# Expert 0's one-hot rows built from 16-bit slot numbers with the channel outermost, and three re-ordered places in the scan stage

## The reference, cut to what matters

```python
# x, ctx: (8, 256, 512); E = 4 experts, H = 2048, capacity 512, TOPK = 2
k, v = layernorm(x), ctx
for t in range(256):                       # one recurrence per sample and channel
    q = max(pp, u + k_t); y_t = (exp(pp-q)*aa + exp(u+k_t-q)*v_t) / (exp(pp-q)*bb + exp(u+k_t-q))
    q2 = max(pp + w, k_t); aa, bb, pp = exp(pp+w-q2)*aa + exp(k_t-q2)*v_t, exp(pp+w-q2)*bb + exp(k_t-q2), q2
x = x + tanh(g_xattn) * y
n = layernorm(x).reshape(2048, 512)
probs = softmax over the top 2 of (n @ Wg + bg)
for i in range(4):                         # the 512 tokens of highest probability for this expert
    sel_p, sel = top_k(where(assigned, probs[:, i], -inf), 512)
    out[sel] += gelu(n[sel] @ W1[i]) @ W2[i] * sel_p
result = x + tanh(g_ffn) * out
```

## Time and profile before

| what | value |
|---|---|
| median of 3 runs | 466.32 us (466.1 to 467.76) |
| profiled execution, its own time | 466.88 us |
| its span | 464.9 us |
| PE busy | 413.6 us, 89% of the span, 2067 matmuls |
| DVE busy | 284.9 us, 61% |
| ACT busy | 313.4 us, 67% |
| POOL busy | 114.1 us, 25% |
| granted TensorE clock, mean | 0.967 |

### The profile page before, as it was taken

How to read it: one execution, slowest core, us unless ns; L and a number is a source line. 1 busy time by engine, 2 the same in 40 slices (tenths; PEclk the granted TensorE clock), 3 DMA queues, 4 the chain that set the end, 5 groups by cost and what they waited for, 6 DMA issues and landing times.

```text
span 464.9 us, 7153 instructions
## 1 busy us (share of the span) xinstructions
PE 413.6 (89%) x2067; PEld 204.7 (44%) x2067; DVE 284.9 (61%) x582; ACT 313.4 (67%) x491; POOL 114.1 (25%) x130
## 2 busy tenths in 40 slices
PE   2598898622999999999999999999999999999992
PEld 1454453311644444444444444444444444444472
DVE  7999898998689966564664183457516435551010
ACT  6798898998589773857878790677879157860000
POOL 0787856602300002520002321100041210001112
PEclk9999999955899999999999999999999999999998
DMA  7985120498600938697002959400095510000212
GB/s 264 356 314 230 41 96 2 183 334 318 184 1 0 362 109 278 130 215 267 0 0 81 362 105 292 156 0 1 13 380 137 79 24 0 0 0 8 38 23 24
DMA packets 36327, 62.80 MB, mean 135 GB/s; under 512 B 14352, under 2 KB 14736, under 8 KB 34256
## 3 DMA queue, kind: packets, MB, share of 16 engines
q1 hardware_dynamic: 32064, 53.32, 33.2%
q0 software_dynamic: 3808, 8.65, 9.4%
q10 hardware_dynamic: 432, 0.54, 0.3%
HBM read 46.78 MB, written 12.58 MB: 128 GB/s over the span
## 4 chain that ended last, share of the span: by engine, by line
PE 72%; DVE 11%; issue 6%; POOL 4%; ACT 3%; DMA 2%; DVEq 0%; POOLq 0%; ACTq 0%
PE ps L870 33%; PE ps L855 27%; PE ps L835 7%; DVE arena L1377 4%; PE ps L883 2%; POOL arena L1222 1%; ACT early L944 1%; DVE arena L1648 1%; DMA rows<-in_L_ffn_W 1%; POOL arena L1213 1%; DMA arena<-xn_table,idx 1%; PE ps L798 1%; DVE arena L1408 1%; DMA small<-in_scalars 1%; DVE arena L1397 1%
## 5 line engine op out<-in xcount | busy, mean ns | idle before, releaser
L870 PE MATMUL ps<-arena 128*128 128x512 f16 x720 | 156.5, 379 | 0.0
L855 PE MATMUL ps<-arena,early 128*128 128x512 f16 x576 | 124.8, 379 | 0.0
L870 PEld LDWEIGHTS ps<-arena 128*128 128x128 f16 x720 | 69.9, 98 | 83.5
L855 PEld LDWEIGHTS ps<-arena,early 128*128 x576 | 56.4, 98 | 68.0
L1119 ACT ACTIVATE arena<-ps,up 128x512 f32<-128x512 f32 x64 | 43.8, 684 | 57.8 <-PE ps L855 40.7
L1827 DVE SCALAR_TENSOR_TENSOR arena<-arena,h_down 128x512 f32 x48 | 36.0, 751 | 58.5 <-ACT arena L1122 58.5
L1298 POOL DMA_INDIRECT result<-arena,idx x15 | 27.7, 1846 | 173.7 <-DVE arena L1855 113.9
L1122 ACT ACTIVATE arena<-arena,h_down 128x512 f32 x64 | 46.2, 722 | 8.7 <-ACT arena L1119 0.2
L1806 DVE SCALAR_TENSOR_TENSOR early<-w_raw,down,early 128x2048 f16<-128x2048 f32 x16 | 37.0, 2345 | 18.8 <-ACT early L1076 18.8
L1125 ACT ACTIVATE arena<-rows,down x64 | 45.2, 706 | 0.0
L1855 DVE TENSOR_SCALAR arena<-ps,yscale 128x512 f32<-128x512 f32 x15 | 11.2, 747 | 50.6 <-PE ps L870 39.3
(11 more groups left out here) (238 smaller groups left out, 483.8 us busy)
## 6 DMA issues: line engine op xcount, KB each, us to landing
w_raw<-in_L_ffn_W SPq DMA_DIRECT2D x4, 4096.0 KB, 13.8
rows<-in_L_ffn_W SPq DMA_DIRECT2D x3, 4096.0 KB, 17.7
rows<-in_L_ffn_W SPq DMA_DIRECT2D x4, 1024.0 KB, 9.9
result<-rows SPq DMA_DIRECT2D x3, 1024.0 KB, 8.6
early<-in_ctx SPq DMA_DIRECT2D x2, 1024.0 KB, 6.1
rows<-in_x SPq DMA_DIRECT2D x2, 1024.0 KB, 10.9
xn_table<-arena SPq DMA_DIRECT2D x4, 512.0 KB, 5.6
xn_table<-arena SPq DMA_DIRECT2D x2, 1024.0 KB, 5.1
```

What stands on the lines that cost most here:

```text
L855: last = nc.tensor.matmul(ps[:, PH[q], :], w[:, k, at], t[:, k, :], start=n == 0, stop=n == 3 * CT - 1)
L870: last = nc.tensor.matmul(ps[:, PY[s % 2], :], h[:, t, s * P:(s + 1) * P], w[:, t, :], start=t == 0 and n == 0, stop=t == HT - 1 and n == 2)
```

## The change

Four edits are made together.

1. **One-hot rows of expert 0.** `hot_0` is laid out with the channel outermost and the token innermost, (128, 16) in place of (16, 128). The slot numbers are int16 (`posi_0`, `slot_a0`, `slot_b0`), and the other operand is a table of int16 channel numbers, each repeated 16 times, in place of the float32 row of `cst`. PE's weights for token t are then `hot_0[:, :, t]`, 128 columns at a distance of 16 elements (32 bytes). Experts 1 to 3 keep their form.
2. **The table's load.** It has 4 KB per partition, 512 KB in all, and lies where the scans' decay factors were. SP issues it behind the last store of normed rows, after a wait for the last scan, and ahead of the second quarter of W2. DVE's one-hot instructions wait for it.
3. **PE's order.** At the first unit of groups 2, 3 and 4 (u = 8, 12, 16), `products(u)` is issued behind the transposes of x, the router's matmul and `keys(u)`, no longer ahead of them.
4. **POOL's and ACT's order.** At units 8 and 11 POOL does `quotient(u)` ahead of `scales1`; at unit 8 ACT does `sums_of_rows` (tile 14) ahead of `exp_rows` (tile 12).

```diff
@@ constants
+C_SLOTS = P * TT // 2
+BEHIND_Q = (8, 11)
@@ constant_table
-    return t
+    slots = np.ascontiguousarray(np.broadcast_to(np.repeat(np.arange(P, dtype=np.int16), TT)[None], (P, P * TT)))
+    return np.ascontiguousarray(np.concatenate([t, slots.view(np.float32)], 1))
@@ tiles
+        hot_0 = part(arena, [at[0]], (P, TT), F16)
         hot = part(arena, at, (TT, P), F16)
+        slot_numbers = part(arena, [HT * D // 2], (P, TT), I16)
+        posi_0 = sb("posi_0", [P, TT], I16)
+        slot_a0 = sb("slot_a0", [P, TT], I16)
+        slot_b0 = sb("slot_b0", [P, TT], I16)
+        def opens(u):
+            return u % CT == 0 and u > CT
@@ SyncE, behind store_xn2(NG - 1) and ahead of first_w2(1, (2,))
+            sp.wait_ge(s_scan, UNITS)
+            sp.dma_start(arena[:, HT * D // 2:HT * D // 2 + C_SLOTS], consts[:, C_ALL:]).then_inc(s_id, 16)
@@ TensorE, the loop over units
-                if u + 2 < UNITS:
+                if u + 2 < UNITS and not opens(u + 2):
                     products(u + 2)
...
                 if long(u):
                     keys(u + 2)
+                if opens(u + 2) and u + 2 < UNITS:
+                    products(u + 2)
@@ TensorE, expert 0's list
-                last = nc.tensor.matmul(ps[:, PI, 0:ST * 4], hot[:, t, :], put[:, 0, t, :], start=t == 0, stop=t == TT - 1)
+                last = nc.tensor.matmul(ps[:, PI, 0:ST * 4], hot_0[:, :, t], put[:, 0, t, :], start=t == 0, stop=t == TT - 1)
@@ ScalarE, the loop over units
                     sums_of_rows(EARLY_A[u])
+                if u in STATS_A and u in BEHIND_Q:
+                    sums_of_rows(STATS_A[u])
                 for t in ROWS_IN.get(u, ()):
                     exp_rows(t)
...
-                if u in STATS_A:
+                if u in STATS_A and u not in BEHIND_Q:
                     sums_of_rows(STATS_A[u])
@@ GpSimd, the loop over units
-                if u in SCALES1:
+                if u in SCALES1 and u not in BEHIND_Q:
                     scales1(SCALES1[u])
                 if u < UNITS - 1:
                     quotient(u)
+                if u in BEHIND_Q:
+                    scales1(SCALES1[u])
@@ VectorE, expert 0's places (slot_b0 and slot_a0 likewise from posi_0)
-            step(nc.vector.scalar_tensor_tensor(posi[:, 0, :], pos[:, 0, 0, :], FAR, pos[:, 1, 0, :], ALU.add, ALU.add))
+            step(nc.vector.scalar_tensor_tensor(posi_0[:, :], pos[:, 0, 0, :], FAR, pos[:, 1, 0, :], ALU.add, ALU.add))
@@ VectorE, slots(e)
+                    if isinstance(e, int) and e == 0:
+                        dve.wait_ge(s_id, 32)
+                        nc.vector.tensor_tensor(hot_0[:, :, half], slot_numbers[:, :, half],
+                                                slot_b0[:, half].unsqueeze(1).to_broadcast([P, P, TT // 2]),
+                                                ALU.is_equal).then_inc(b_hot, 1)
+                        continue
                     nc.vector.tensor_tensor(hot[:, half, :],
                                             cst[:, C_IOTA:C_IOTA + P].unsqueeze(1).to_broadcast([P, TT // 2, P]),
                                             slot_b[:, e, half].unsqueeze(2).to_broadcast([P, TT // 2, P]),
                                             ALU.is_equal).then_inc(b_hot, 1)
```

More of the change, by code:

```diff
@@ L58 @@
 I32 = mybir.dt.int32
+I16 = mybir.dt.int16
 U32 = mybir.dt.uint32
@@ L192, in part @@
             cols = math.prod(dims)
-            words = cols * (2 if dt in (F16, BF16) else 4) // 4
+            words = cols * (2 if dt in (F16, BF16, I16) else 4) // 4
             v = home[:, at[0]:at[0] + words]
@@ L522, in _ @@
             sp.dma_start(c_sb[:, a:b, :], rows_of(c_v, a, b)).then_inc(s_c[1], 16)
-            sp.dma_start(cst[:, C_TRI:], consts[:, C_TRI:]).then_inc(s_cst, 16)
+            sp.dma_start(cst[:, C_TRI:], consts[:, C_TRI:C_ALL]).then_inc(s_cst, 16)
             a, b = FIRST[2], FIRST[3]
@@ L1689, in _ @@
                                                 flags[:, :, 0, :], ALU.add, ALU.mult))
-            step(nc.vector.scalar_tensor_tensor(posi[:, 0, :], pos[:, 0, 0, :], FAR, pos[:, 1, 0, :], ALU.add, ALU.add))
-            nc.vector.tensor_scalar(slot_b[:, 0, :], posi[:, 0, :], P - 1, None, ALU.bitwise_and).then_inc(b_dve, 1)
-            step(nc.vector.tensor_scalar(slot_a[:, 0, :], posi[:, 0, :], 7, None, ALU.logical_shift_right), 2)
-            step(nc.vector.tensor_tensor(in_a[:, 0, :, :], slot_a[:, 0, :].unsqueeze(2).to_broadcast([P, TT, ST]),
+            step(nc.vector.scalar_tensor_tensor(posi_0[:, :], pos[:, 0, 0, :], FAR, pos[:, 1, 0, :], ALU.add, ALU.add))
+            nc.vector.tensor_scalar(slot_b0[:, :], posi_0[:, :], P - 1, None, ALU.bitwise_and).then_inc(b_dve, 1)
+            step(nc.vector.tensor_scalar(slot_a0[:, :], posi_0[:, :], 7, None, ALU.logical_shift_right), 2)
+            step(nc.vector.tensor_tensor(in_a[:, 0, :, :], slot_a0[:, :].unsqueeze(2).to_broadcast([P, TT, ST]),
                                          cst[:, C_IOTA:C_IOTA + ST].unsqueeze(1).to_broadcast([P, TT, ST]), ALU.is_equal))
@@ L1985 @@
     arrays["in_constants"] = constant_table()
-    args.append(nc.dram_tensor("in_constants", (P, C_ALL), F32, kind="ExternalInput").ap())
+    args.append(nc.dram_tensor("in_constants", (P, C_ALL + C_SLOTS), F32, kind="ExternalInput").ap())
     args.append(nc.dram_tensor("result", (BATCH, SEQ, D), F32, kind="ExternalOutput").ap())
```

## The result

The changed kernel takes 463.99 us (median of five, 463.22 to 464.69) where the kernel before takes 466.32. That is 2.3 us less by the medians. The ratio is 0.9933, with a 95% interval from 0.9915 to 0.9952, which is 3.1 us less, between 2.2 and 4.0 us: two of the five runs before took 467.76 and 468.07 us, which the median leaves out. The forecast was 463.5 us in a range from 462.9 to 465.4. The profiled execution took 463.88 us where that of before took 466.88, 3.0 us less against the 2.8 us of the forecast's sum. The sum was nearly met; its terms were not, as the rows show.

What follows compares the result with a forecast made beforehand. PE, 72% of the chain's span, multiplies without a gap from about 130 us, so only that start can move: 2.0 us (scan stage) + 0.8 (one-hot part) = 2.8, median 463.5 us, range 462.9 to 465.4.

Steps and rivals of the forecast that it cites:

- What bounds the kernel, and unit 8: Scan stage: DVE waits for POOL's quotient; reordering gains 0.4 us ahead of unit 8 plus its 1.31 us wait, 1.7 us.
- What is late next: Unit 9: quotient starts at 52.1 us, a new DVE wait of about 1.2 us leaves some 0.5 of 1.7 us.
- Unit 11: Scan stage: scales of tiles 14 and 15 change places with the quotient; 0.75 us of the 0.84 us wait gained.
- unit 15: Scan stage: router and keys ahead let `add_first(15)` move earlier; 0.8 us of the residual's 1.41 us wait gained.
- Scan stage in sum: Last scan 2.0 us earlier, from 0.5 + 0.75 + 0.8; bounds 1.0 and 2.6 us.
- One-hot instructions: DVE, routing stage: two elements a step, 0.69 us each in place of 1.216; the pair 1.29 us.
- PE's loads: Expert 0's list matmuls: loads at 0.05 us, 0.07 at most, list 0.95 us earlier; no gain at 0.134 us.
- The table: SP's 512 KB load lands at 110.7 us, just ahead of the one-hot instructions; 0.1 us of waiting counted.
- What of it reaches PE: Expert 0's start: 0.85 us at the gathers; PE's waits at L712 and L835, 0.4 us each, go: 0.8 us.
- The rival "the one-hot part gives nothing": Routing stage: one-hot edits leave the list at its old time; 464.3 us, chance 0.20.

Runs made afterwards that it cites:

- the first trace: Profiled execution of the changed kernel, all four edits, in its first measurement: 463.88 us against 466.88 us for the kernel before.
- the second: The changed kernel measured again, unaltered: 463.42 us, ratio 0.9928 against the kernel before.
- the table-ahead one: Changed kernel with the table issued ahead of the last two stores of normed rows instead of behind them: 463.40 us, ratio 0.9936 against the kernel before.
- one-hot only: Kernel before with only the 16-bit one-hot rows and the table's load, scan stage as before: 466.06 us, ratio 1.0.

## Why the prediction came out right, step by step

- **What bounds the kernel, and unit 8.** Right in kind. PE's order was worth more ahead of unit 8 than the 0.4 us I took: I capped it by DVE's waits at the residuals and left out that scans wait too: 0.28 us at the scan below, of the kernel before, which starts at 41.42, just behind PE's `keys(8)` (to 41.34). The mis-sized term is "DVE can gain no more than it idled there, 0.44 us": 0.92 us were gained, the 0.76 us of waits and some short gaps.

```profile
41.42 2.29 DVE L1377 TENSOR_TENSOR_SCAN arena<-arena,ps 128x1024 f32<-128x1024 f32 x1 [0.28 <-issue]
```

- **What is late next.** Confirmed: quotient 9 at 51.99 (predicted 52.1), its wait 1.39 us (1.2), net gain at unit 9 0.76 us (0.5).
- **Unit 11** gave 0.92 us (0.75), **unit 15** 1.0 us (0.8). What is left there is the way round: from the copy behind the scan (71.63 us) over PE, ACT and POOL to the residual at 75.87 are 4.2 us, and DVE's own work in this stretch, with its short scan, ends at 75.47.
- **Scan stage in sum:** 2.68 us against 2.0. The shares of the edits were not those I gave: edit 3 alone is worth 2.2 us, edit 4 is worth 0.5 on top of it and nothing alone.
- **One-hot instructions:** 159 + 528 = 687 ns forecast, 688 measured.
- **PE's loads:** taken at 0.05 to 0.07 us, measured 0.080. That is below the 0.134 at which it would have turned. The Trainium skill, "Advanced Engine Details and Errata", section "SBUF Cachelines", has the direction right: 163 against 106 ns for the step of 32 bytes. From the first one-hot start to `idx` it takes 110.58 - 108.51 = 2.07 us instead of 113.64 - 110.81 = 2.83: 0.76 us less, where I had taken 0.95.
- **The table** landed 0.3 us late in the first trace and 0.2 us early in the second. In the first the pair starts 108.51, 2.30 us earlier than before and not 2.68: 0.38 us lost where 0.1 was taken. 0.76 - 0.38 leaves the list 0.38 us better than the scan stage makes it, not 0.85.
- **What of it reaches PE** is the step that failed. The prediction named the real limit, warm-up matmuls that wait for W1's high halves and do not come earlier with the list, and then did not use it. It said that PE waited 0.4 us at L712 and 0.4 us at L835 and that an earlier list takes out 0.8. The row at L835 is one of PEld, as its own name says: the weight load waits while PE still multiplies. The changed kernel has the same wait at L852 (0.4 us), and its matmuls of L815 run from 126.88 for 3.62 us, to 130.50, when L852 starts at 130.45. There was nothing to take out. And the wait at L712 hangs on W2's last quarter, whose landing took 5.5 to 6.9 us in the traces whatever the list did. Of 0.8 us, 0.2 came in the first trace and 0.4 in the table-ahead one; one-hot only has a ratio of 1.0 and leaves room for 0.5 us at most.
- So the forecast's 2.8 us were met by luck, out of two errors that nearly cancel: 0.7 us too little in the scan stage and 0.6 too much behind it (by the first trace). The rival "the one-hot part gives nothing" was nearer in what the one-hot part gave, but in none of the three ways that it named (one element a step, loads at 0.13 us, a table one microsecond late): the list did end earlier, and PE had little use for it.

Open stays why W2's last quarter lands in 5.5 us once and in 6.9 another time; no run isolates it.

## What to carry to other kernels

When a stage is a ring of engines, look for work that waits for a slow producer and stands ahead of work that does not: moving it behind cost nothing that the runs show and gave 2.2 of the 2.7 us. Moving a critical instruction ahead of its neighbours on a loaded engine only pays if the neighbours' readers have slack; here it paid nothing alone, and 0.5 us once the waits ahead of it were gone. Before pricing an earlier result, list everything else that joins behind it (another engine's halves, a transfer) and when each is ready, and read a weight load's wait only together with PE's own row.

## What was not expected of the hardware

- DVE writing 16-bit elements 256 bytes apart took 4828 ns for 1024 elements, (4828 - 159) / 1024 = 4.6 ns each; the same inputs written to neighbours took 688 ns. The Trainium skill, "Advanced Engine Details and Errata", section "SBUF Cachelines", speaks of a penalty for an access on another line and gives no size; here it is sevenfold for DVE's writes and 1.5-fold for the time of a weight load (32 bytes apart).
- A step of zero innermost costs DVE its two elements a step even with 16-bit types (1222 ns against 688), while the same repetition one dimension further out does not. The Trainium skill, "VectorE: DVE Perf Modes", section "What auto-detection actually checks", asks for step 1 in every tensor; both runs agree with it. For the output stepped by 256 bytes the rule would leave one element a step, which is an estimate of 2.4 us the pair by the 1222 ns; the run shows 9.3.
- A 1 MB load issued behind the first of four gathers made the slowest gather land 6.2 us after its issue in place of 3.8; behind the second it did not (3.9 us). Each is one trace.
